# Seam between cross attention and experts: order of the last values, logits and combine weights, earlier splits, and the order of the last pair

## The chip, the cores and the metric

One core of a Trainium2 chip runs the whole kernel in one launch. The metric is the device time in microseconds (us). The engines are TensorE (PE: matrix products and transposes), VectorE (DVE), ScalarE (ACT), GpSimd (POOL) and SyncE (SP), which here only issues the transfers between main memory and on-chip memory. Each engine runs its own list of instructions in order; semaphores make one engine wait for another.

## The reference, cut to what matters

One decoder layer on x of shape (16, 128, 256) in float32, with three residual stages:

```python
x = x + attention(layernorm(x))                    # compressed, selected and window attention
x = x + cross(layernorm(x), context)               # 8 heads, each softmax(q k^T) v over features
x = x + experts(layernorm(x))                      # top 8 of 64 experts, and a shared one

# experts
probs = softmax(x @ gate_w)
topk_w, topk_idx = top_k(probs, 8);  topk_w /= sum(topk_w)
combine = zeros(T, 64).at[arange(T)[:, None], topk_idx].add(topk_w)
for e in range(64):
    out += combine[:, e, None] * ((silu(x @ gw[e]) * (x @ uw[e])) @ dw[e])
out += sigmoid(x @ shared_gate) * shared(x)
```

The kernel computes every expert for every token and weighs it with `combine`, which is zero where an expert was not chosen.

## The kernel before

**Cross attention** goes batch by batch (`B` = 16) through `cross_tensor`, `cross_scalar`, `cross_vector` and `cross_pool`, which list each engine's work in the order in which it runs. A batch has eight score matmuls (u = 0 to 7) whose exponentials ScalarE takes (L1531). `values(b, 0)` and `values(b, 1)` (L1468) are 32 small matmuls that multiply probabilities and values; `keep_pv` (ScalarE, L1546) copies the sums out of their bank; `turn_values` (L1481) transposes them into the bank `XOUT`; `normalised` (VectorE, L1569 and L1571) divides; `turn_back` (L1487) transposes again into the same bank; `residual` (VectorE, L1577) adds to `X`; `next_stats` (L214) begins the next layer norm.

**Routing** takes the batches in four groups of four. `route_turn` (PE, L1686) and `route_split` (VectorE, L1695 and L1697) turn a normalised batch and split it into a high and a low part, because every float32 product is made of three matmuls in the fp32r format (high by high, high by low, low by high). The low parts are made by GpSimd (L1672). `route_logits` (PE, L1707) makes the logits of a batch, `route_keep` (VectorE, L1716) stores them, `route_choose` finds the eight largest (L1730 to L1738), `route_exps` (ScalarE) takes exponentials, `route_weights` (VectorE, L1750 to L1758) makes the combine weights, `route_turn_weights` (PE, L1767) transposes them, `route_keep_weights` (ScalarE, L1774) copies them to `combineT`. SyncE then writes `combineT` to main memory (L1812) and reads single rows back, spread over 64 partitions each, as `comb` (L1817). Of the first pair's `comb`, the half for tokens 0 to 511 needs group 0 and the half for tokens 512 to 1023 needs group 1.

**Experts** are taken as 33 pairs in each of two passes over 1024 tokens, pairs n = 0 to 65; the last pair of a pass holds the shared expert and has only half of the products up. Each pair has two halves h of 512 tokens. On PE, `moe_up` (L1893; L1886 for the shared expert) makes the gate product (side 0) and the up product (side 1) of a half, six matmuls each, and `down` (L1909) twelve matmuls of a half. The PE order is, for a pair n: up(n, 0), down(n-1, 0), up(n, 1), down(n-1, 1). Between them lie, for each half: SiLU on ScalarE (`gate`, L2009), product with the up side on VectorE (`gated`, L2052 into `act_u`; L2050 for the shared expert), product with `comb` on GpSimd (`weigh`, L2109 into `hidden`), the high part on ScalarE (L2015), the low part on VectorE (`hidden_low`, L2057). The weights are split too: high parts on ScalarE (`moe_up_high` L1997, `down_high` L2021), low parts on GpSimd (`moe_up_low` L2099, `down_low` L2114). The hidden values and the weights meet in `down`, which waits for `down_split` and `h_ready`.

In pairs 1 to 13 VectorE also carries the routing of the second eight batches. In pair 1 its order is: gated(1, 0), hidden_low(0, 1), `ln_close` (L245 to L254, the reciprocal square root of the layer norm of batches 8 to 15), gated(1, 1), hidden_low(1, 0), `route_normal` of batch 8 (L259). In pair 2 PE needs that batch for `route_turn` (L1686), which stands between up(2, 0) and down(1, 0).

The order at the seam on PE is `route_logits(7)`, `route_turn_weights(0)`, `turn_values(14)`, `values(15)`, `turn_back(14)`, then the first pair's products up, with `turn_values(15)`, `turn_back(15)` and `route_turn_weights(1)` among them (L1508 to L1522).

Of the kernel before, what the change touches and what calls it, by code (L numbers as in the profile page):

```python
# [8 lines left out]
ALU = mybir.AluOpType  # L9
# [57 lines left out]
def build(nc, io):  # L67
    ctx = ExitStack()
    with ctx:
# [1365 lines left out]
        def cross_tensor(pe):  # L1435
# [56 lines left out]
            for i in range(B):  # L1492
                for u in range(XH):
# [13 lines left out]
                    route_cross_tensor(pe, i, u)  # L1507
            route_logits(pe, 7)  # L1508
            route_turn_weights(pe, 0)
            turn_values(B - 2)  # L1510
            values(B - 1, 0)
            values(B - 1, 1)
            turn_back(B - 2)
            pe.wait_ge(S("x_lo_ready"), ROUTED)
# [3 lines left out]
            moe_up(pe, 0, 0, 0, 0, (1,))  # L1518
            turn_back(B - 1)
            route_turn_weights(pe, 1)  # L1520
            pe.wait_ge(S("x_lo_ready"), 2 * ROUTED)
            moe_up(pe, 0, 0, 0, 1)  # L1522


        def cross_scalar(act):
# [22 lines left out]
            for i in range(B):  # L1548
                for u in range(XH):
                    softmax(i, u)  # L1550
                    if u == 3 and i + 1 < B:
                        cross_keep_shift(act, i + 1)
                    if u == 0 and i + 4 < B:
                        cross_query_high(act, i + 4)
                    if u == 7:
                        keep_values(i)
                    if u == 6 and 0 <= i - 1 < B:
                        keep_pv(i - 1)
                    route_cross_scalar(act, i, u)
            route_keep_weights(act, 0)  # L1560
            keep_pv(B - 1)
            route_exps(act, 1)


        def cross_vector(dve):
# [26 lines left out]
            for i in range(B):  # L1592
# [9 lines left out]
                for u in range(XH):  # L1602
                    if i + 2 < B:
                        cross_reduce_max(dve, i + 2, u)
                    if u == 2 and 0 <= i - 2 < B:
                        normalised(i - 2)
                    if u == 6 and 0 <= i - 2 < B:
                        residual(i - 2)
                    if u == 7 and 0 <= i - 2 < B:
                        next_stats(i - 2)  # L1610
                    route_cross_vector(dve, i, u)
            route_keep(dve, 7)
# [3 lines left out]
            next_stats(B - 2)  # L1616
            normalised(B - 1)
            residual(B - 1)
            route_weights(dve, 1)
            next_stats(B - 1)  # L1620


        def cross_pool(pool):
# [8 lines left out]
            moe_up_low(pool, 0, 0)  # L1632
            route_low_pool(pool, 2 * ROUTED - 1)


# [147 lines left out]
        def route_cross_vector(dve, i, u):  # L1783
# [5 lines left out]
            if (i, u) == (15, 1):  # L1789
                route_choose(dve, 0)  # L1790
            if (i, u) == (15, 5):
                route_weights(dve, 0)

# [103 lines left out]
        def moe_tensor(pe):  # L1897
# [63 lines left out]
            with pe.Fori(0, (PAIRS - 3) // 2) as i:  # L1961
                slot(2 * i + PAIRS + 2, 1, PASS)
                slot(2 * i + PAIRS + 3, 0, PASS)
            slot(LAST, 1, PASS)
            down(LAST, 1, 0)
# [23 lines left out]
        def moe_up_high(act, n, p, ps=0):  # L1989
# [7 lines left out]
            nc.scalar.copy(out, src).then_inc(S("up_hi_ready"), 1)  # L1997

        def moe_scalar(act):
            def up_high(n, p, ps):  # L2000
# [10 lines left out]
            def hidden_high(n, h):  # L2011
                act.wait_ge(S(f"weighed{h}"), n + 1)
                if not isinstance(n, int) or n:
                    act.wait_ge(S("down_done"), 2 * n - 1 + h)
                nc.scalar.copy(h_hi[h][:], hidden[h][:]).then_inc(S(f"h_hi_ready{h}"), 1)  # L2015

            def down_high(n, p):
                act.wait_ge(S(f"ld_down{p}"), 8 * (n - p) + 16)
                if not isinstance(n, int) or n > 1:
                    act.wait_ge(S("down_done"), 2 * n - 2)  # L2020
                nc.scalar.copy(down_hi[p][:], down_in[p][:]).then_inc(S("down_hi_ready"), 1)  # L2021

            def pair(n, p, ps):
# [3 lines left out]
                if not isinstance(n, int) or n:  # L2027
                    hidden_high(n - 1, 1)
                if not isinstance(n, int) or n < LAST:
                    up_high(n + 1, 1 - p, ps)  # L2030
                gate(n, 1)
                if isinstance(n, int) and n in (7, 11):
# [3 lines left out]
                hidden_high(n, 0)  # L2036
                down_high(n, p)

# [4 lines left out]
        def moe_vector(dve):  # L2043
# [16 lines left out]
            def pair(n, p, ps):  # L2060
# [8 lines left out]
                if route:  # L2069
                    route_keep(dve, n + 6)  # L2070
                gated(n, 1, ps)
                if route:
                    route_low(dve, n + 6)
# [22 lines left out]
        def moe_up_low(pool, n, p):  # L2096
            pool.wait_ge(S("up_hi_ready"), n + 1)
            out, src = up_parts(n, up_lo, p)
            nc.gpsimd.tensor_tensor(out, src, up_parts(n, up_hi, p)[0], ALU.subtract).then_inc(S("up_split"), 1)  # L2099

        def moe_pool(pool):
            def weigh(n, p, h):
# [8 lines left out]

            def down_low(n, p):
                pool.wait_ge(S("down_hi_ready"), n + 1)
                nc.gpsimd.tensor_tensor(down_lo[p][:], down_in[p][:], down_hi[p][:], ALU.subtract)\  # L2114
                    .then_inc(S("down_split"), 1)

            def pair(n, p, ps):
                first = isinstance(n, int) and n == 0
                if first:
                    moe_up_low(pool, 1, 1)  # L2120
                weigh(n, p, 0)
                if not first and (not isinstance(n, int) or n < LAST):
                    moe_up_low(pool, n + 1, 1 - p)
                weigh(n, p, 1)
                down_low(n, p)

# [197 lines left out]
```

## Time and profile before

| | |
|---|---|
| median of 3 runs | 1142.57 us (1141.6 to 1144.57) |
| the profiled execution | 1139.89 us |
| its span, first to last instruction | 1138.1 us |
| mean granted TensorE clock | 0.987 of full |
| PE busy | 1068.4 us, 94% |
| VectorE, ScalarE, GpSimd busy | 641.2, 544.4, 639.5 us |
| products up (L1893), three groups of 512 matmuls | 203.4 + 202.4 + 202.0 us |
| products down (L1909), three groups of 528 matmuls | 150.7 + 149.8 + 149.6 us |

The expert stage begins at 557.3 us of the span, with the first matmul of L1893. Cross attention ends around it. A busy time is a sum over an engine's instructions; an engine's idle time matters only if the engine is the one that others wait for at that point. Matmuls are pipelined, so each row's duration overlaps with the next row's start: what a matmul costs is the distance from one start to the next.

### The profile page before, as it was taken

To read this page: it belongs to the slowest core of one execution; us is meant where nothing else is said; L and a number is where in the kernel's file an instruction comes from. 1 tells how busy PE (TensorE), PEld (TensorE's weight loads), DVE (VectorE), ACT (ScalarE), POOL (GpSimd) and SP (SyncE) were. 2 spreads that over 40 slices of the span, in tenths; PEclk is the share of its full clock that TensorE was granted. 3 is DMA by queue.
4 is the path that set the end of the run, shared out by engine and by line. 5 is a ranking of instruction groups with operands and counts; after the bars stand their busy time and mean duration, and the time that the engine had idled before them with its cause. 6 is when DMAs were issued, how large, how long until landed. Compare 5 with 4: busy or idle time off the path is not lost.

```text
span 1138.1 us, 22315 instructions
## 1 busy us (share of the span) xinstructions
PE 1068.4 (94%) x7447; PEld 873.8 (77%) x7480; DVE 641.2 (56%) x1453; ACT 544.4 (48%) x1142; POOL 639.5 (56%) x773
## 2 busy tenths in 40 slices
PE   5979999999999989999799999999999999999997
PEld 4757767777777766766578888888888888888886
DVE  7756777677777779887667643333233323332333
ACT  2326656666666647776433443333343333333332
POOL 4685665656668522222355556665666666656664
PEclk9979999999999999999999999999999999999999
DMA  5201111111100156672143333434435334344342
GB/s 136 66 1 28 31 30 39 32 39 28 40 25 20 38 112 141 155 168 67 40 128 98 98 102 105 126 99 108 118 98 159 105 102 124 97 110 116 97 120 70
DMA packets 75231, 97.10 MB, mean 85 GB/s; under 512 B 20540, under 2 KB 55996, under 8 KB 75148
## 3 DMA queue, kind: packets, MB, share of 16 engines
q1 hardware_dynamic: 75148, 96.05, 32.0%
q8 instruction: 45, 0.74, 0.3%
q14 instruction: 38, 0.31, 0.1%
HBM read 82.73 MB, written 13.12 MB: 84 GB/s over the span
## 4 chain that ended last, share of the span: by engine, by line
PE 56%; DVE 5%; ACT 2%; issue 1%; POOL 0%; POOLq 0%; DVEq 0%; ACTq 0%
PE bank L1893 30%; PE bank L1909 16%; PE bank L1468 2%; PE bank L1443 2%; PE bank L1366 2%; DVE xmax L1376 1%; ACT probs L1531 1%; PE bank L1707 1%; PE bank L1481 1%; PE bank L1886 0%; DVE h_lo L2057 0%; ACT act_g L2009 0%; PE bank L1686 0%; POOL hidden L2109 0%; ACT xpv L1546 0%
## 5 line engine op out<-in xcount | busy, mean ns | idle before, releaser
L2109 POOL TENSOR_TENSOR hidden<-act_u,comb 128x512 f32<-128x512 f32 x132 | 210.5, 1595 | 220.5 <-DVE act_u L2052 152.3
L2052 DVE TENSOR_TENSOR act_u<-act_g,bank 128x512 f32<-128x512 f32 x128 | 88.0, 688 | 335.2 <-ACT act_g L2009 167.6
L2009 ACT ACTIVATE act_g<-bank 128x512 f32<-128x512 f32 x132 | 79.0, 599 | 340.3 <-PE bank L1893 340.2
L1893 PE MATMUL bank<-x_hi,up_hi 128*128 128x512 f32 x512 | 203.4, 397 | 0.1
L1893 PE MATMUL bank<-x_hi,up_lo 128*128 128x512 f32 x512 | 202.4, 395 | 0.0
L1893 PE MATMUL bank<-x_lo,up_hi 128*128 128x512 f32 x512 | 202.0, 394 | 0.0
L1909 PE MATMUL bank<-down_hi,h_hi 128*128 128x256 f32 x528 | 150.7, 285 | 6.3 <-POOL down_lo L2114 6.3
L870 ACT ACTIVATE probs<-bank 128x512 f32<-128x512 f32 x192 | 113.8, 604 | 82.8 <-PE bank L682 45.7
L1909 PE MATMUL bank<-down_hi,h_lo 128*128 128x256 f32 x528 | 149.8, 284 | 0.0
L1909 PE MATMUL bank<-down_lo,h_hi 128*128 128x256 f32 x528 | 149.6, 283 | 0.0
L1893 PEld LDWEIGHTS bank<-x_hi,up_lo 128*128 128x128 f32 x512 | 96.3, 188 | 22.5
L1909 PEld LDWEIGHTS bank<-down_hi,h_hi 128*128 128x128 f32 x528 | 100.8, 191 | 13.6 <-POOL down_lo L2114 8.2
L1893 PEld LDWEIGHTS bank<-x_lo,up_hi 128*128 128x128 f32 x512 | 96.9, 189 | 17.6
L1893 PEld LDWEIGHTS bank<-x_hi,up_hi 128*128 128x128 f32 x512 | 97.1, 190 | 17.0 <-issue 0.3
L2057 DVE TENSOR_TENSOR h_lo<-hidden,h_hi 128x512 fp32r<-128x512 f32 x132 | 103.5, 784 | 7.6 <-ACT h_hi L2015 7.6
L1909 PEld LDWEIGHTS bank<-down_lo,h_hi 128*128 128x128 f32 x528 | 100.8, 191 | 4.8
L1909 PEld LDWEIGHTS bank<-down_hi,h_lo 128*128 128x128 f32 x528 | 101.2, 192 | 0.0
L2099 POOL TENSOR_TENSOR up_lo<-up_in,up_hi 128x512 fp32r<-128x512 f32 (+1 forms) x66 | 87.6, 1328 | 12.2 <-ACT up_hi L1997 12.2
L1531 ACT ACTIVATE probs<-bank 128x512 f32<-128x512 f32 x128 | 75.4, 610 | 39.3 <-PE bank L1443 39.0
L993 DVE TENSOR_REDUCE blockmax<-bank 128x32 f32<-128x512 f32 x96 | 64.7, 689 | 50.6 <-PE bank L632 31.8
L1376 DVE TENSOR_REDUCE xmax<-bank 128x2 f32<-128x512 f32 x128 | 82.3, 683 | 13.7 <-PE bank L1366 13.2
L680 PE MATMUL bank<-query,keys 128*128 128x256 f32 x256 | 84.2, 352 | 0.5 <-ACT probs L870 0.4
(268 smaller groups left out, 2195.7 us busy)
## 6 DMA issues: line engine op xcount, KB each, us to landing
comb<-combine_scratch SPq DMA_DIRECT2D x130, 256.0 KB, 3.8
up_in<-in_w_up SPq DMA_DIRECT2D x66, 256.0 KB, 3.6
down_in<-in_w_down SPq DMA_DIRECT2D x66, 128.0 KB, 3.7
keys_x<-key_rows_x SPq DMA_DIRECT2D x32, 192.0 KB, 3.3
ctx_in<-in_ctx SPq DMA_DIRECT2D x32, 128.0 KB, 2.1
key_rows_x<-ctx_hi SPq DMA_DIRECT2D x256, 16.0 KB, 1.5
query_x<-xq_rows_hi SPq DMA_DIRECT2D x64, 64.0 KB, 3.2
key_rows_x<-ctx_lo SPq DMA_DIRECT2D x128, 16.0 KB, 1.5
```

What stands on the lines that cost most here:

```text
L680: nc.tensor.matmul(o, keys[p][:, kvh * 4 + j, :], query[p][:, kvh, 256:512], start=True, stop=False)
L870: nc.scalar.activation(probs[:, u, :], SCORE[u % 2][:], ACT.Exp, scale=SCALE)\
L993: ins = nc.vector.tensor_reduce(blockmax[:, s, :, c0:c0 + 4], SMAX[m % 2][:].rearrange("p (h c k) -> p h c k", h=KV, k=BLK), AX, ALU.max)
L1376: nc.vector.tensor_reduce(xmax[b % 2][:, m // 4, hs:hs + 2], XMAX[(XH * b + m) % 3][:].rearrange("p (h n) -> p h n", h=2), AX, ALU.max).th ...
L1531: nc.scalar.activation(probs4[b % 2][:, u, :], XSCORE[n % 2][:], ACT.Exp, scale=XSCALE)\
L1893: last = nc.tensor.matmul((GATE, UP)[s][h][:], wp[p][:, c, s, :], xp[:, c, t:t + 512], start=k == 0, stop=k == 5)
L1909: last = nc.tensor.matmul(OUT[k // 2][:, k % 2 * D:k % 2 * D + D], hp[h][:, q * 128:q * 128 + 128], wp[p][:], start=False, stop=True, skip ...
L2009: nc.scalar.activation(act_g[h][:], GATE[h][:], ACT.Silu).then_inc(S(f"gated{h}"), 1)
L2052: ins = nc.vector.tensor_tensor(act_u[h][:], act_g[h][:], UP[h][:], ALU.mult)
L2057: nc.vector.tensor_tensor(h_lo[h][:], hidden[h][:], h_hi[h][:], ALU.subtract)\
L2099: nc.gpsimd.tensor_tensor(out, src, up_parts(n, up_hi, p)[0], ALU.subtract).then_inc(S("up_split"), 1)
L2109: nc.gpsimd.tensor_tensor(hidden[h][:], act_u[h][:], comb[p][:, 512 * h:512 * h + 512], ALU.mult)\
```

## The change

On PE, `values(15)` and `turn_values(14)` go ahead of `route_logits(7)` and `route_turn_weights(0)`; `route_turn_weights(1)` goes behind the gate side of the first pair's second half. On VectorE, `route_weights(0)` leaves its place at (i, u) = (15, 5) and goes behind the last `route_split`, `next_stats` goes behind the `route_split` of the same step, and `route_weights(1)` goes ahead of `residual(15)`. On ScalarE, the high parts of pair 1's weights up and pair 0's weights down are made in the cross stage, and `keep_pv(15)` stands ahead of `route_keep_weights(0)`. On GpSimd, their low parts are made right after the last `route_low_pool`. In the last pair, PE makes both halves up before the two halves down of the pair before; ScalarE splits the down weights between the two SiLUs; VectorE instead of GpSimd makes the product with `comb` for the second half.

```diff
@@ cross_tensor
-            route_logits(pe, 7)
-            route_turn_weights(pe, 0)
             turn_values(B - 2)
             values(B - 1, 0)
             values(B - 1, 1)
+            route_logits(pe, 7)
+            route_turn_weights(pe, 0)
             turn_back(B - 2)
...
             turn_back(B - 1)
+            pe.wait_ge(S("x_lo_ready"), 2 * ROUTED)
+            moe_up(pe, 0, 0, 0, 1, (0,))
             route_turn_weights(pe, 1)
-            pe.wait_ge(S("x_lo_ready"), 2 * ROUTED)
-            moe_up(pe, 0, 0, 0, 1)
+            moe_up(pe, 0, 0, 0, 1, (1,))
@@ cross_scalar
+            moe_up_high(act, 1, 1)
+            moe_down_high(act, 0, 0)
+            keep_pv(B - 1)
             route_keep_weights(act, 0)
-            keep_pv(B - 1)
             route_exps(act, 1)
@@ cross_vector
+                    route_cross_vector(dve, i, u)
                     if u == 7 and 0 <= i - 2 < B:
                         next_stats(i - 2)
-                    route_cross_vector(dve, i, u)
+            route_weights(dve, 0)
             route_keep(dve, 7)
             normalised(B - 2)
             route_choose(dve, 1)
             residual(B - 2)
             next_stats(B - 2)
             normalised(B - 1)
+            route_weights(dve, 1)
             residual(B - 1)
-            route_weights(dve, 1)
             next_stats(B - 1)
@@ cross_pool
             route_low_pool(pool, 2 * ROUTED - 1)
+            moe_up_low(pool, 1, 1)
+            moe_down_low(pool, 0, 0)
@@ route_cross_vector
-            if (i, u) == (15, 5):
-                route_weights(dve, 0)
@@ moe_tensor
-            slot(LAST, 1, PASS)
+            up(LAST, 1, PASS, 0)
+            up(LAST, 1, PASS, 1)
+            down(LAST - 1, 0, 0)
+            down(LAST - 1, 0, 1)
             down(LAST, 1, 0)
             down(LAST, 1, 1)
@@ moe_scalar (down_high is now moe_down_high, outside it)
             def hidden_high(n, h):
-                act.wait_ge(S(f"weighed{h}"), n + 1)
+                if isinstance(n, int) and n == LAST and h:
+                    act.wait_ge(S("last_weighed"), 1)
+                else:
+                    act.wait_ge(S(f"weighed{h}"), n + 1)
...
-                if not isinstance(n, int) or n < LAST:
+                if not isinstance(n, int) or 0 < n < LAST:
                     up_high(n + 1, 1 - p, ps)
+                last = isinstance(n, int) and n == LAST
+                if last:
+                    moe_down_high(act, n, p)
                 gate(n, 1)
...
-                down_high(n, p)
+                if not last and (not isinstance(n, int) or n):
+                    moe_down_high(act, n, p)
@@ moe_vector
                 gated(n, 1, ps)
+                if isinstance(n, int) and n == LAST:
+                    dve.wait_ge(S("ld_comb1"), 16 * LAST + 16)
+                    dve.wait_ge(S("upped1"), LAST + 1)
+                    nc.vector.tensor_tensor(hidden[1][:], act_u[1][:], comb[1][:, 512:1024], ALU.mult)\
+                        .then_inc(S("last_weighed"), 1)
@@ moe_pool (down_low is now moe_down_low, outside it)
-                if first:
-                    moe_up_low(pool, 1, 1)
                 weigh(n, p, 0)
                 if not first and (not isinstance(n, int) or n < LAST):
                     moe_up_low(pool, n + 1, 1 - p)
-                weigh(n, p, 1)
-                down_low(n, p)
+                if not isinstance(n, int) or n < LAST:
+                    weigh(n, p, 1)
+                if not first:
+                    moe_down_low(pool, n, p)
```

## Rows read from the trace of the kernel before

**Rows 1.** Windows: busy us (instructions) of each engine, granted clock, DMA share, GB/s.

```profile
552.20:554.70 2.50, 2.50 (x12) 2.11 (x12) 0.30 (x2) 0.58 (x1) 0.72 (x1) 0.55 0.02 7
...
561.00:563.30 2.30, 0.03 (x2) 0.01 (x1) 2.11 (x8) 0.00 (x0) 0.00 (x0) 1.00 0.00 0
...
572.80:575.50 2.70, 2.67 (x12) 2.67 (x13) 2.67 (x3) 0.62 (x1) 2.48 (x2) 0.52 0.78 187
...
690.00:790.00 100.00, 100.00 (x572) 87.53 (x572) 30.94 (x48) 35.76 (x71) 61.76 (x48) 1.00 0.40 110
```

**Rows 2.** Timeline of TensorE at the seam: start us, duration us, instruction [idle before].

```profile
552.20 0.92 PE L1707 MATMUL bank<-w_router,xnT 128*128 128x65 f32 x4 [3.17 <-DVE xnT L1697]
...
554.75 2.45 PE L1468 MATMUL bank<-probs,xvalue 128*32 128x256 f32 x32
...
558.80 0.60 PE L1481 MATMUL bank<-ident,xpv 128*128 128x128 f32 x4
...
563.29 0.63 PE L1767 MATMUL bank<-ident,combine 128*66 128x128 f32 x4 [2.27 <-DVE combine L1758]
...
572.83 0.53 PE L1909 MATMUL bank<-down_hi,h_hi 128*128 128x256 f32 x1 [2.43 <-POOL down_lo L2114]
...
582.92 0.38 PE L1686 MATMUL bank<-ident,xn 128*128 128x128 f32 x2
```

**Rows 3.** Timeline of ScalarE at the seam.

```profile
549.56 0.37 ACT L1539 COPY xvalue<-bank 128x256 f32<-128x256 f32 x1
...
563.96 0.58 ACT L1774 COPY combineT<-bank 66x512 f32<-66x512 f32 x1 [3.12 <-PE bank L1767]
```

**Rows 4.** Timeline of VectorE at the seam and in pairs 0 and 1.

```profile
549.03 1.40 DVE L1756 TENSOR_TENSOR combine<-chosen,route_s 128x256 f32<-128x256 f32 x1
...
555.50 0.22 DVE L1730 MAX8 top<-logits 128x8 f32<-128x64 f32 x1
...
557.68 0.42 DVE L1577 TENSOR_TENSOR X<-X,bank 128x256 f32<-128x256 f32 x1
...
561.39 0.42 DVE L1750 TENSOR_TENSOR chosen<-chosen,route_e 128x256 f32<-128x256 f32 x1
...
563.05 0.18 DVE L1758 RECIPROCAL combine<-route_e 128x4 f32<-128x4 f32 x1
...
572.78 0.69 DVE L2057 TENSOR_TENSOR h_lo<-hidden,h_hi 128x512 fp32r<-128x512 f32 x1 [2.29 <-ACT h_hi L2015]
...
574.68 1.20 DVE L247 TENSOR_SCALAR rstd<-rstd 128x8 int32<-128x8 int32 x1
...
577.52 0.17 DVE L254 SCALAR_TENSOR_TENSOR rstd<-newton,rstd 128x8 f32<-128x8 f32 x1
...
580.26 1.38 DVE L259 TENSOR_SCALAR xn<-X,mean,rstd 128x256 f32<-128x256 f32 x1
```

**Rows 5.** Timeline of GpSimd at the seam and in pairs 0 and 1.

```profile
548.88 1.26 POOL L2099 TENSOR_TENSOR up_lo<-up_in,up_hi 128x512 fp32r<-128x512 f32 x1
...
570.84 1.26 POOL L2109 TENSOR_TENSOR hidden<-act_u,comb 128x512 f32<-128x512 f32 x1 [3.16 <-DMA comb<-combine_scratch]
...
579.82 1.67 POOL L2109 TENSOR_TENSOR hidden<-act_u,comb 128x512 f32<-128x512 f32 x1 [3.97 <-DVE act_u L2052]
...
581.45 0.78 POOL L2114 TENSOR_TENSOR down_lo<-down_in,down_hi 128x256 fp32r<-128x256 f32 x1
```

**Rows 6.** Timeline of TensorE in the last pair.

```profile
1130.74 0.38 PE L1909 MATMUL bank<-down_hi,h_hi 128*128 128x256 f32 x1 [2.99 <-POOL down_lo L2114]
```

**Rows 7.** Timeline of GpSimd in the last pair.

```profile
1124.88 1.62 POOL L2109 TENSOR_TENSOR hidden<-act_u,comb 128x512 f32<-128x512 f32 x1 [1.70 <-issue]
1128.36 1.65 POOL L2109 TENSOR_TENSOR hidden<-act_u,comb 128x512 f32<-128x512 f32 x1 [1.86 <-DVE act_u L2050]
1129.97 0.72 POOL L2114 TENSOR_TENSOR down_lo<-down_in,down_hi 128x256 fp32r<-128x256 f32 x1
```

**Rows 8.** Timeline of VectorE in the last pair.

```profile
1127.60 0.68 DVE L2050 TENSOR_TENSOR act_u<-act_g,act_u 64x512 f32<-64x512 f32 x1 [2.25 <-ACT act_g L2009]
```

More of the change, by code:

```diff
@@ L1997, in moe_up_high, with moe_down_high @@
             nc.scalar.copy(out, src).then_inc(S("up_hi_ready"), 1)
+        def moe_down_high(act, n, p):
+            act.wait_ge(S(f"ld_down{p}"), 8 * (n - p) + 16)
+            if not isinstance(n, int) or n > 1:
+                act.wait_ge(S("down_done"), 2 * n - 2)
+            nc.scalar.copy(down_hi[p][:], down_in[p][:]).then_inc(S("down_hi_ready"), 1)
         def moe_scalar(act):
@@ L2015, in hidden_high @@
                 nc.scalar.copy(h_hi[h][:], hidden[h][:]).then_inc(S(f"h_hi_ready{h}"), 1)
[L2017 to L2021, printed above, removed]
             def pair(n, p, ps):
@@ L2099, in moe_up_low, with moe_down_low @@
             nc.gpsimd.tensor_tensor(out, src, up_parts(n, up_hi, p)[0], ALU.subtract).then_inc(S("up_split"), 1)
+        def moe_down_low(pool, n, p):
+            pool.wait_ge(S("down_hi_ready"), n + 1)
+            nc.gpsimd.tensor_tensor(down_lo[p][:], down_in[p][:], down_hi[p][:], ALU.subtract)\
+                .then_inc(S("down_split"), 1)
         def moe_pool(pool):
@@ L2110, in weigh @@
                     .then_inc(S(f"weighed{h}"), 1)
[L2112 to L2115, printed above, removed]
             def pair(n, p, ps):
                 first = isinstance(n, int) and n == 0
-                if first:
-                    moe_up_low(pool, 1, 1)
                 weigh(n, p, 0)
```

## The prediction

> **What bounds the kernel now.** I read the page's busy shares first: PE is the only engine near full. Then windows: in the loops of the expert stage PE is busy 100.00 of 100 us, nothing of this change touches the work there, and PE waits for nobody [rows 1]. So the change can only win or lose at the seam and at the end. Next the timeline of PE there. It shows four gaps: 3.17 us before the last logits, ended by VectorE's `xnT`; 2.27 us before the second transposes of combine weights; 2.43 us before the first product down [rows 2]; 2.99 us before the last pair's product down [rows 6]. The windows add the clock: behind the first and the third gap the granted clock was 0.55 and 0.52, the 1.2 GHz level, and behind the second it stayed at 1.00 [rows 1]. Last I read the other engines' timelines, to see what would be late once these gaps close.
>
> All times below are on the axis of the profiled span, those of the changed kernel carried over from rows of before. PE's own pace comes from the loop window: 572 matmuls in 100 us [rows 1], half of them over 512 columns and half over 256, so 0.233 and 0.117 us each; six wide ones are 1.4 us, twelve narrow ones 1.4.
>
> **Seam, first part: up to the second transposes of combine weights.** PE ends its last score at 552.20 - 3.17 = 549.03 [rows 2]. Before, VectorE made combine weights ahead of the last split, and PE's logits hung on that. Now PE does `turn_values(14)` at once (its inputs, `xpv` and `residual(13)`, are there about then), and `values(15)` from 550.0, when ScalarE's `xvalue` has ended (549.56 + 0.37) [rows 3]. The 32 matmuls took 2.38 us (554.75 to 557.13), partly at the low clock; I take 2.1, so 552.1, and the logits end at about 552.65 (under the 0.92 of their row) [rows 2].
>
> VectorE meanwhile: split and `next_stats` to about 550.1, then `route_weights(0)`. Its cost with GpSimd idle is 561.39 to 563.23, 1.84 us [rows 4]. But its L1756 took 1.40 us at 549.03 while GpSimd's L2099 ran from 548.88 to 550.14 [rows 4, 5]; the normal size of such a product over 256 columns is the 0.42 of L1750. The two engines exclude each other. The change puts three more GpSimd products right there: the last x_lo, the low part of pair 1's weights up (1.26) and of pair 0's weights down (0.78) [rows 5], about 2.75 us in a row. Bounds for the end of `route_weights(0)`: 551.95 (no collision) and 553.7 (two collisions of about 0.9). I take 553.15. Then logits kept, `normalised(14)` (0.7) and `turn_back(14)` at 554.15.
>
> The Trainium skill ("SBUF — State Buffer", section "SBUF: two separate sides") has it as a rule that speaks against this part: a VectorE operation with two inputs in SBUF and a GpSimd operation that reads SBUF lock each other out for the whole instruction. The trace agrees, with the 1.40 us above. By the rule in full the end would be 553.7; without it 551.95.
>
> Next a new order bites. `turn_values(15)` needs `residual(14)`, which stands behind `route_choose(1)` on VectorE. Choosing takes from 555.50 to about 557.55, and the residual comes at 557.68 [rows 4]. New: 554.1 + 2.0 = 556.1, residual until 556.5. PE has finished the gate side of half 0 by 555.8 and waits 0.7 us. `turn_values(15)` comes at 556.5 instead of 558.80 [rows 2]: 2.3 us sooner. Behind it PE issues 0.47 of transposes, 1.4 for six matmuls up, 0.23 for `turn_back(15)` and, by the change, another 1.4 for the gate side of half 1, so `route_turn_weights(1)` can start at 560.0. Its weights are ready at 557.8 + 1.84 = 559.65. It started at 563.29 [rows 2]. Gain at this point 3.25 us; the 2.27 us gap is gone, since other work lies in it.
>
> **Seam, second part: the chain through memory.** PE then runs ahead: the rest of the first pair, up(1, 0) until 564.7, the sums started, and down(0, 0) without a wait, because pair 0's weights down are split long before and its hidden values ready at about 563.6. The 2.43 us gap is gone too, and the clock should stay up. But the second half's `comb` still goes ScalarE copy, write, read: from 563.29 to 570.84, 7.55 us [rows 2, 5]. Nothing shortens that; it shifts to 560.05 + 7.55 = 567.6. VectorE's low part of hidden(0, 1) came 1.94 later, at 572.78 [rows 4]: now 569.55, so down(0, 1) starts at 570.3 where PE would be ready at 569.85. That is 8.4 us ahead of the old order, but it does not last. Behind this low part stands `ln_close` on VectorE, which ended at 577.52 + 0.17, 4.91 us after the low part's start, 1.0 of it a wait for GpSimd in L247 [rows 4]. Before, this lay under PE's own work. Now it ends at 569.55 + 4.91 = 574.45, then gated(1, 1), hidden_low(1, 0), and batch 8's normalised rows (L259, 1.38, from 580.26) [rows 4], at 574.45 + 0.7 + 0.6 + 1.4 = 577.15. PE stands ready for `route_turn(8)` at 575.45 (up(2, 0) begins at 572.65, since the second `comb` and the low part of pair 2's weights arrive 3.25 us sooner, not 8), and waits 1.7 us. It ran at 582.92 [rows 2]. GpSimd's `weigh(1, 1)` and `down_lo` (1.67 and 0.78) [rows 5] end at 577.7, and down(1, 0) needs that. It began at 583.08 (582.92 and two transposes). **So 583.08 - 577.7 = 5.4 us are kept.** From there every pair has the phases of before, since PE is the bound. Bounds for this term: below 3.25 less 0.5, if the end of the chain slips as the VectorE and GpSimd products collide in another order; above 7.5, if VectorE's chain is 2 us shorter and PE's own arrival sets it. 5.4 is what the rows' own distances give.
>
> **The end.** Before, the last product down of half 0 waited for hidden(65, 1) and then `down_lo`, both on GpSimd: 1128.36 + 1.65, 1129.97 + 0.72, start at 1130.74 [rows 6, 7]. Now `down_lo` comes right behind hidden(65, 0), 1124.88 + 1.62 = 1126.50 [rows 7], and half 1's SiLU ends at about 1125.95 instead of 1127.57, since up(65, 1) has moved 2.1 us forward on PE. VectorE then has gated(65, 1), blocked to 1126.50, done 1127.05; GpSimd's `down_lo` to 1127.75; the product with `comb` to 1128.35 (sized by its 0.68 neighbour, L2050 [rows 8]); and only then the low part of half 0, which used to be ahead of it in time: 1128.95. Half 1's own low part ends at 1129.7, before PE needs it. PE starts at 1129.0, **1.75 us sooner**. Bounds: 2.9 without any collision, 0.8 with one more of each 1 us.
>
> **Sum.** 5.4 + 1.75 = 7.15 us of the profiled execution's 1139.89, so 1132.7. That execution lies 2.7 below the median of 1142.57, which is what is to be predicted: 1142.57 - 7.15 = 1135.4, say 1135.3. What is costed at nothing: PE's matmuls, which are the same; ScalarE's two early casts, in its idle time before the first combine weights; no transfer is added, and SyncE's order is unchanged.
>
> **Rivals.**
> 1. PE itself sets the restart (the chain through `ln_close` is shorter, because the blocked L247 of 1.20 and L259 of 1.38 [rows 4] would take some 0.2 each where they meet no GpSimd product): 7.5 + 2 to 2.9, about 10 us, 1132.5. For it: both depend on phase alone. Against: GpSimd's products follow the same event, so they shift along.
> 2. The clock falls again. The new waits of PE between 569.8 and 577.7 are about 0.45, 0.9 and 2.0 us; a gap of 2.43 was followed by 0.52, one of 2.27 was not [rows 1, 2]. At the low clock twelve narrow matmuls filled 2.67 us [rows 1] where the pace above gives 1.4, and some three wide ones behind them cost as much again as they take, 0.6: about 1.9 us a time. Gain 7.15 - 1.9 = 5.2, with a second fall 3.3: 1137.4 to 1139.3.
> 3. No change to be seen: `route_weights(0)` beside three GpSimd products ends so late that the second transposes win only 1 us, and the tail's collisions take another 1: gain 3 or less, 1140.
> 4. Slower. The loops leave with other phases, and in every pair the product down waits for `weigh` or `h_lo`, which now collide. It would decide from 7.15/65 = 0.11 us a pair; at 0.2 a pair it costs 13, and 1148 results. Against it: 100.00 of 100 us busy, with GpSimd at 61.76 [rows 1], so about a third of its time is slack, and a PE bound loop pulls the phases back.
>
> **How the numbers follow.** Forecast 0.48, rival 1 0.20, rival 2 0.20, rival 3 0.08, rival 4 0.04. The measurement can tell about 0.3%, 3.4 us, from no change, so faster means below 1139.1: the forecast, rival 1 and most of rival 2, 0.87; same 0.09; slower 0.04. The range 1131.2 to 1139.3 holds the forecast, rivals 1 and 2 and the scatter of the medians, where 1141.6 to 1144.57 was seen.
>
> **What would show it.** Right: no gap above 1 us on PE between 549 and 564, the second transposes (L1767) about 3.2 us sooner, L1893 back to back until the zero matmuls, a wait of 1 to 2 us before L1686 of batch 8 ended by VectorE's `xn`, the granted clock at 1.00 from 549 to 580, and a last gap of about 2 us. Wrong: L1756 at its 0.42 and no wait before L1686 (rival 1), a window at half clock (rival 2), or waits of PE in the loop windows (rival 4).

## The result and the profile after

| | before | changed |
|---|---|---|
| median of 19 runs each | 1141.62 us (1139.28 to 1148.21) | 1137.62 us (1132.01 to 1141.42) |
| ratio, with 95% interval | | 0.9954 (0.9938 to 0.9969) |
| the profiled execution, and its span | 1139.89, 1138.1 us | 1132.01, 1130.2 us |
| mean granted clock of that execution | 0.987 | 0.990 |

Faster, by about 5 us in the runs and by 7.9 us from one profiled execution to the other. A later series gave 0.9933 (0.9920 to 0.9945). Why trace and runs differ is the main thing the experiments had to settle.

TensorE's timeline at the seam in the changed kernel (start, duration, instruction, idle before). L1481 is `turn_values`, L1773 `route_turn_weights`, L1692 `route_turn`, L1897 a product up; it answers to [rows 2].

```profile
548.32 0.39 PE L1692 MATMUL bank<-ident,xn 128*128 128x128 f32 x2
...
548.87 0.65 PE L1481 MATMUL bank<-ident,xpv 128*128 128x128 f32 x4
549.89 1.93 PE L1468 MATMUL bank<-probs,xvalue 128*32 128x256 f32 x32 [0.37 <-ACT xvalue L1540]
...
553.28 0.63 PE L1773 MATMUL bank<-ident,combine 128*66 128x128 f32 x4 [0.86 <-DVE combine L1764]
...
556.52 0.63 PE L1481 MATMUL bank<-ident,xpv 128*128 128x128 f32 x4 [0.68 <-DVE X L1580]
...
560.01 0.60 PE L1773 MATMUL bank<-ident,combine 128*66 128x128 f32 x4
...
569.76 0.34 PE L1913 MATMUL bank<-down_hi,h_hi 128*128 128x256 f32 x1
...
573.24 0.50 PE L1897 MATMUL bank<-x_hi,up_hi 128*128 128x512 f32 x1 [1.82 <-POOL up_lo L2118]
...
576.59 0.41 PE L1692 MATMUL bank<-ident,xn 128*128 128x128 f32 x2 [0.29 <-DVE xn L259]
...
586.11 0.38 PE L1692 MATMUL bank<-ident,xn 128*128 128x128 f32 x2
```

The three gaps of [rows 2] are gone. What is left: 0.37, 0.86 and 0.68 us behind single waits, a new gap of 1.82 before up(2, 0), and 0.29 before batch 8's transposes. The second transposes of combine weights come at 560.01 instead of 563.29, batch 8's at 576.59 instead of 582.92.

VectorE there, against [rows 4]:

```profile
550.99 1.41 DVE L1762 TENSOR_TENSOR combine<-chosen,route_s 128x256 f32<-128x256 f32 x1
552.32 0.69 DVE L1763 TENSOR_SCALAR route_e<-route_e 128x4 f32<-128x4 f32 x1
...
568.98 0.69 DVE L2071 TENSOR_TENSOR h_lo<-hidden,h_hi 128x512 fp32r<-128x512 f32 x1 [3.38 <-ACT h_hi L2031]
...
570.20 1.16 DVE L252 SCALAR_TENSOR_TENSOR newton<-newton,var_eps 128x8 f32<-128x8 f32 x1
...
572.00 1.22 DVE L254 SCALAR_TENSOR_TENSOR rstd<-newton,rstd 128x8 f32<-128x8 f32 x1
...
575.05 1.39 DVE L259 TENSOR_SCALAR xn<-X,mean,rstd 128x256 f32<-128x256 f32 x1
```

and GpSimd, against [rows 5]:

```profile
549.93 0.95 POOL L1678 TENSOR_TENSOR x_lo<-xnT,x_hi 128x256 fp32r<-128x256 f32 x1
550.85 1.27 POOL L2118 TENSOR_TENSOR up_lo<-up_in,up_hi 128x512 fp32r<-128x512 f32 x1
552.08 0.90 POOL L2122 TENSOR_TENSOR down_lo<-down_in,down_hi 128x256 fp32r<-128x256 f32 x1
...
566.99 1.30 POOL L2133 TENSOR_TENSOR hidden<-act_u,comb 128x512 f32<-128x512 f32 x1 [4.55 <-DMA comb<-combine_scratch]
...
571.92 1.26 POOL L2118 TENSOR_TENSOR up_lo<-up_in,up_hi 128x512 fp32r<-128x512 f32 x1 [0.59 <-ACT up_hi L2004]
```

L1762 ends 0.28 us after GpSimd's up_lo (552.40 against 552.12), L1763 0.03 us after its down_lo (553.01 against 552.98). In `ln_close` two operations of eight columns take 1.16 and 1.22 us beside two GpSimd products of 512 columns. From the second transposes to the product with half 1's `comb` it is 566.99 - 560.01 = 6.98 us (7.55 before).

The last pair: TensorE, VectorE, GpSimd, against [rows 6 to 8].

```profile
1122.93 0.36 PE L1913 MATMUL bank<-down_hi,h_hi 128*128 128x256 f32 x1 [1.82 <-DVE h_lo L2071]
```

```profile
1120.09 0.96 DVE L2064 TENSOR_TENSOR act_u<-act_g,act_u 64x512 f32<-64x512 f32 x1 [0.74 <-ACT act_g L2022]
1121.15 1.03 DVE L2089 TENSOR_TENSOR hidden<-act_u,comb 128x512 f32<-128x512 f32 x1
1122.11 1.46 DVE L2071 TENSOR_TENSOR h_lo<-hidden,h_hi 128x512 fp32r<-128x512 f32 x2
```

```profile
1118.88 1.62 POOL L2133 TENSOR_TENSOR hidden<-act_u,comb 128x512 f32<-128x512 f32 x1 [1.68 <-issue]
1120.47 1.17 POOL L2122 TENSOR_TENSOR down_lo<-down_in,down_hi 128x256 fp32r<-128x256 f32 x1
```

From batch 9's transposes to the last products down, 538.59 us before (592.15 to 1130.74), it is now 536.82: 1.77 less, and all of that in the last pair: its first product up begins 529.09 us behind batch 9's transposes before and 529.13 after.

### The profile page after: what moved, and what is told of

Its sections match the earlier page's. It is cut to its first block, busy times and chain, and to the rows that moved or that the text cites. A ratio compares the mean times of both kernels' runs of the same rounds, so it can differ in the third digit from the quotient of the medians.

```text
span 1130.2 us, 22316 instructions
## 1 busy us (share of the span) xinstructions
PE 1068.4 (95%) x7447; PEld 873.1 (77%) x7480; DVE 642.5 (57%) x1454; ACT 544.4 (48%) x1142; POOL 638.0 (56%) x772
## 4 chain that ended last, share of the span: by engine, by line
PE 52%; DVE 4%; issue 3%; ACT 2%; POOL 2%; DMA 1%; SPq 1%; DVEq 0%; ACTq 0%; POOLq 0%
PE bank L1897 29%; PE bank L1913 16%; PE bank L1443 2%; PE bank L1468 2%; PE bank L1366 1%; ACT probs L1532 1%; POOL xn L1673 1%; DVE xmax L1376 0%; POOL x_lo L1678 0%; DMA comb<-combine_scratch 0%; DVE h_lo L2071 0%; PE bank L1481 0%; PE bank L1890 0%; PE bank L1713 0%; SPq L1312 0%
## 5 line engine op out<-in xcount | busy, mean ns | idle before, releaser
L1897 PE MATMUL bank<-x_hi,up_hi 128*128 128x512 f32 x512 | 203.3, 397 | 1.9 <-POOL up_lo L2118 1.8
L1897 PE MATMUL bank<-x_hi,up_lo 128*128 128x512 f32 x512 | 202.5, 395 | 0.0
L1897 PE MATMUL bank<-x_lo,up_hi 128*128 128x512 f32 x512 | 201.8, 394 | 0.0
L1897 PEld LDWEIGHTS bank<-x_hi,up_lo 128*128 128x128 f32 x512 | 96.2, 188 | 22.5
L1897 PEld LDWEIGHTS bank<-x_hi,up_hi 128*128 128x128 f32 x512 | 96.9, 189 | 18.8 <-POOL up_lo L2118 2.0
L1897 PEld LDWEIGHTS bank<-x_lo,up_hi 128*128 128x128 f32 x512 | 96.7, 189 | 17.6
```

What stands on the lines that cost most here:

```text
L1897: last = nc.tensor.matmul((GATE, UP)[s][h][:], wp[p][:, c, s, :], xp[:, c, t:t + 512], start=k == 0, stop=k == 5)
```

## The experiments

Nine kernels, the changed one among them, were timed beside the kernel before, and there is one more trace each of the kernel before, the changed one and splits_only. To compare their traces I use four lengths: A, from the first instruction to the last `route_turn` transposes of the cross stage (548.32 above), in which the kernels differ only in VectorE's order (`next_stats` behind `route_split`, and where the first combine weights begin); the seam, from there to batch 9's transposes (586.11 above); the stretch from there to the last products down; and the rest of the span. The first three come from the same three rows of TensorE's timeline. In the traces that have 8.5 us or more to the end, the granted clock fell to 0.50 behind TensorE's last gap or in the products that follow it.

| trace | A | seam | to last down | to the end | median us, ratio to before |
|---|---|---|---|---|---|
| before | 548.41 | 43.74 | 538.59 | 7.4 | |
| before_again | 548.52 | 43.19 | 538.57 | 9.5 | one run |
| changed | 548.32 | 37.79 | 536.82 | 7.3 | 0.9954 (0.9938 to 0.9969) |
| after_again | 554.28 | 39.20 | 536.80 | 7.3 | 1135.0, 0.9933 (0.9920 to 0.9945) |
| after_third | 551.33 | 37.84 | 536.77 | 7.4 | one run |
| seam_only | 552.49 | 37.90 | 538.58 | 8.7 | 1139.3, 0.9964 (0.9951 to 0.9977) |
| tail_only | 550.07 | 43.53 | 536.77 | 8.7 | 1141.5, 0.9993 (0.9981 to 1.0005) |
| splits_only | 550.20 | 41.31 | 538.57 | 8.7 | 1142.9, 1.0004 (0.9990 to 1.0018) |
| splits_again | 554.97 | 41.05 | 538.60 | 9.6 | one run |
| late_splits | 550.77 | 39.36 | 536.80 | 8.6 | 1138.0, 0.9958 (0.9943 to 0.9972) |
| apart | 548.13 | 38.30 | 536.78 | 7.3 | 1135.0, 0.9940 (0.9923 to 0.9957) |
| tuned | 550.14 | 35.89 | 536.77 | 8.5 | 1133.9, 0.9919 (0.9905 to 0.9932) |
| tuned2 | 551.51 | 35.49 | 536.21 | 7.6 | 1133.4, 0.9923 (0.9906 to 0.9940) |
| fill | 552.67 | 37.86 | 536.78 | 7.4 | 1136.6, 0.9940 (0.9917 to 0.9962) |

**after_again.** The changed kernel, unaltered.

> The changed kernel, unaltered, for a second trace. The two profiled spans differ by 7.9 us (1138.1 and 1130.2), but the timed runs only by a ratio of 0.9954 (0.9938 to 0.9969), some 5.2 us, and its 19 runs spread from 1132.0 to 1141.4 with mean granted clocks from 0.990 down to 0.980. Theory A (clock): runs differ in how long TensorE is at its 1.2 GHz level; time follows the clock at about 10 us per 0.01, and a trace at 1136 or more has half-clock windows that the first one lacked, either somewhere before 545 us (common to both kernels) or between 569 and 578 us, where the gap of 1.82 us stands. Theory B (memory): the chain copy, write, read of the combine weights varies; then the time between the second transposes (L1773) and the product with comb of half 1 (L2133) is not 7.0 us but 9 or more, with the clock at 0.990. Ratio to before expected 0.9954, between 0.993 and 0.998.

Measured: span 1137.6 at a clock of 0.982. The length A is 6 us longer than in the first trace of the same kernel, and there is more half clock in it, most of it early; windows of the first trace and of this one:

```profile
50.00:100.00 50.00, 41.18 (x329) 31.65 (x329) 30.25 (x63) 18.82 (x44) 38.28 (x72) 0.80 0.07 18
```

```profile
50.00:100.00 50.00, 41.68 (x315) 32.17 (x313) 28.32 (x59) 17.14 (x40) 35.85 (x71) 0.73 0.06 16
...
581.00:587.00 6.00, 6.00 (x31) 5.11 (x30) 3.89 (x6) 1.62 (x3) 3.65 (x4) 0.78 0.55 151
```

Between 300 and 400 us the granted clock was 0.97, where the first trace had 1.00. Another 1.4 us are lost in the seam, in a longer gap before up(2, 0) and at the half clock behind it:

```profile
579.80 0.50 PE L1897 MATMUL bank<-x_hi,up_hi 128*128 128x512 f32 x1 [2.52 <-POOL up_lo L2118]
```

Theory A holds; the chain of theory B took 6.88 us here (565.96 to 572.84), no more than in the first trace. The clock's part can be estimated from the runs, each of which has its mean granted clock c. The clock has two levels, so time at the half clock is 2(1-c) times the time. Over the 149 runs that have their clock on record, a straight line within each kernel gives 0.33 us of time per us at half clock. With that part taken out the scatter (standard deviation) of the kernel before (54 runs) falls from 1.8 to 0.8 us and that of the changed one (26) from 2.5 to 0.7, and the kernel before stands at 1130.3, 1130.4 and 1130.2 in the runs timed beside the three later sets:

| | mean us | us at half clock | mean with that part out (error) |
|---|---|---|---|
| before | 1142.9 | 38.5 | 1130.3 (0.1) |
| changed | 1136.8 | 33.9 | 1125.6 (0.1) |
| seam_only | 1139.1 | 34.9 | 1127.6 (0.2) |
| tail_only | 1141.7 | 39.8 | 1128.7 (0.2) |
| splits_only | 1143.2 | 40.3 | 1129.9 (0.2) |
| late_splits | 1137.8 | 34.7 | 1126.4 (0.3) |
| apart | 1135.1 | 30.3 | 1125.2 (0.3) |
| tuned | 1133.4 | 29.8 | 1123.5 (0.2) |
| tuned2 | 1133.6 | 30.6 | 1123.5 (0.3) |
| fill | 1136.8 | 34.5 | 1125.5 (0.3) |

So the change is worth 6.2 us (error 0.5) in the mean of these runs, from the unrounded means. By this estimate 4.7 of them are there with the clock's part out, and 1.5 come through 4.6 us (error 1.4) less at half clock. This takes it that half clock costs the same wherever it lies. Lines through single kernels have slopes of 0.22 to 0.40, which would make the 4.7 anything from 5.2 to 4.3.

**seam_only and tail_only.** The two halves of the change alone; for the first:

```diff
-            up(LAST, 1, PASS, 0)
-            up(LAST, 1, PASS, 1)
-            down(LAST - 1, 0, 0)
-            down(LAST - 1, 0, 1)
+            slot(LAST, 1, PASS)
```

and ScalarE, VectorE and GpSimd of that pair as before; the second is the same edit the other way, in the kernel before.

> The changed kernel with the last pair as before. Theory: seam and end are independent terms. The traces put 6.0 us on the seam and 1.8 on the end, so this kernel should be 1.8 us slower than the changed one, with a last gap on TensorE of 3.0 us again, and the seam up to 580 us as in the changed kernel. Ratio to before 0.9965 if the timed gain is 5.2 us in all, 0.9948 if the seam is worth its 6.0. Rival: the end is worth nothing in time, because the closing stores start when they started before; then it equals the changed kernel.

> The kernel before with only the last pair reordered. Theory: 1.8 us faster than before, ratio 0.9984; last gap on TensorE 1.8 us in place of 2.99, product of half 1 on VectorE delayed by GpSimd's low part to about 1.0 us, its seam unchanged with gaps of 3.17, 2.27 and 2.43. Rival: 0, ratio 1.000.

Measured: with the clock part out, the end is worth 1130.3 - 1128.7 = 1.6 us and the seam 1130.3 - 1127.6 = 2.7 (error 0.2 each), together 4.3 of 4.7: the terms add up. The traces have the end at 1.8 in both (538.58 against 536.8). The intervals of the ratios hold the forecasts of 0.9984 and 0.9965, but tail_only's holds 1 too, so the end's gain shows only with the clock part out, where the rival (the end is worth nothing) falls.

**splits_only and splits_again.** The early splits without the new orders: 

```diff
+            moe_up_high(act, 1, 1)
+            moe_down_high(act, 0, 0)
             route_keep_weights(act, 0)
...
             route_low_pool(pool, 2 * ROUTED - 1)
+            moe_up_low(pool, 1, 1)
+            moe_down_low(pool, 0, 0)
```

> The kernel before with the early splits of pair 1's weights up and pair 0's weights down alone; all orders on TensorE and VectorE, and the last pair, as before. Counted from the last transposes of route_turn in the cross stage (548.41 before, 548.32 after) to those of batch 9 (592.15 and 586.11): before 43.74 us, changed 37.79. Theory: the 2.43 us gap before the first product down and the half clock behind it go, but the chain copy, write, read of half 1's comb and ln_close keep their place; from batch 8's normalised rows (L259, ready at 581.64 at the earliest) TensorE is late again. It starts at 3.17 + 2.27 us of gaps as before, gains 2 to 2.5 us: 41.5. Rival: the gap simply closes in full with its clock and all that follows keeps up: 43.74 - 2.43 - 1.9 = 39.4. Rival 2: another late thing swallows it, 43.7.

> The early splits alone once more. Its first trace was 2.4 us shorter in the seam than the kernel before (41.31 against 43.74), 1.9 of that from a half-clock stretch that was missing, but its runs were not faster (ratio 1.0004, 0.9990 to 1.0018). Theory: the missing stretch was a matter of that execution; in others TensorE falls to 1.2 GHz behind another gap, and only about 0.5 us are kept: 41.3 to 43.5 for the interval. Rival: 41.3 again, and the timed runs lose the 2.4 us elsewhere, in a place where its code is that of the kernel before.

Measured: 41.31 where 41.5 was forecast, and 41.05, just below the 41.3 to 43.5 of the second. As expected the wait moved: in the first trace the first product down no longer waits, the transposes of batch 8 do.

```profile
581.99 0.41 PE L1690 MATMUL bank<-ident,xn 128*128 128x128 f32 x2 [1.35 <-DVE xn L259]
```

But the runs are not faster (1.0004), and with the clock part out 0.4 us are left (error 0.3). The other 2 us of the traces are not found in the runs; the half clock was 40.3 us (error 2.3) against 38.5. The second trace shows a fall behind the 2.27 us gap, where both traces of before had none:

```profile
557.00:569.00 12.00, 8.85 (x64) 5.88 (x64) 7.38 (x33) 4.42 (x11) 2.65 (x3) 0.86 0.14 35
569.00:575.00 6.00, 5.13 (x18) 4.12 (x19) 1.70 (x7) 1.69 (x3) 1.28 (x1) 0.72 0.12 38
```

The first trace of before, behind its gap of 2.27:

```profile
557.00:569.00 12.00, 9.73 (x51) 7.64 (x48) 6.30 (x18) 6.52 (x14) 2.54 (x2) 1.00 0.17 47
```

The seam of splits_again is short all the same. TensorE did not wait before its transposes of batch 8 (586.79), so it seems that the slower products took the time of that wait.

**late_splits.** The new orders without the early splits; the four pieces of work go back to pair 0. The part in the cross stage:

```diff
-            moe_up_high(act, 1, 1)
-            moe_down_high(act, 0, 0)
...
-            moe_up_low(pool, 1, 1)
-            moe_down_low(pool, 0, 0)
```

> The changed kernel without the early splits: pair 1's weights up and pair 0's weights down are split in pair 0 as before; the new orders and the new last pair stay. Theory: pair 1's low part is ready 1.2 us after TensorE wants it, and the product down of pair 0 waits for GpSimd behind the second half's product with comb, a gap of about 3 us before 569 with half the clock behind it: from the last route_turn transposes of the cross stage to those of batch 9 39.5 to 41.5 us instead of 37.79. Rival: since the chain through memory sets the restart anyway, the early splits are worth nothing: 37.8. Second rival: without three GpSimd products beside it route_weights(0) is 1 us shorter, so it is faster than the changed kernel, 37.

Measured: 39.36, 1.6 us more than the changed kernel (the forecast began at 39.5), with two gaps, and a fall of the granted clock behind the second (0.50 from 572.8 to 574.8):

```profile
564.94 0.50 PE L1893 MATMUL bank<-x_hi,up_hi 128*128 128x512 f32 x1 [1.12 <-POOL up_lo L2114]
...
570.81 0.38 PE L1909 MATMUL bank<-down_hi,h_hi 128*128 128x256 f32 x1 [1.94 <-POOL down_lo L2118]
```

and 0.8 us more (error 0.3) with the clock part out. Alone the early splits give 0.4, on top of the new orders 0.8, of 2.7 for the seam: the orders carry most of it.

**apart.** The early low parts wait for the second combine weights.

```diff
+            pool.wait_ge(S("combine_ready"), 2)
             moe_up_low(pool, 1, 1)
             moe_down_low(pool, 0, 0)
```

> The changed kernel, with one wait more: the two early low parts on GpSimd start only when the second combine weights are made, so they no longer stand beside route_weights(0). Theory: L1762 and L1763 take 0.43 and 0.17 us instead of 1.41 and 0.69, combine weights 0 are ready 1.5 us sooner, and the whole VectorE chain behind them (choose, residual, weights 1) with it, of which the second transposes win 0.9 to 1.4 us; from the last route_turn transposes to L1773's second 10.5 instead of 11.69, and to those of batch 9 about 36.8 instead of 37.79. Rival: TensorE's own order holds it (it waited only 0.86 and 0.68 us), gain 0.7 or less, and the late low parts now delay the first products: 37.8 to 38.5.

Measured: the collision is gone,

```profile
550.80 0.43 DVE L1763 TENSOR_TENSOR combine<-chosen,route_s 128x256 f32<-128x256 f32 x1
551.15 0.17 DVE L1764 TENSOR_SCALAR route_e<-route_e 128x4 f32<-128x4 f32 x1
```

and the second transposes stand 11.04 us behind the start of the interval (559.17 - 548.13) where they stood 11.69. But the seam is 38.30, not 36.8: the gap before up(2, 0) is 2.39 and the clock fell behind it. The rival had the size right: 1.5 us of VectorE's wait for GpSimd cost TensorE 0.65 up to there, and 0.4 (error 0.3) in the runs with the clock part out.

**tuned and tuned2.** What the trace of the changed kernel shows as late, moved ahead:

```diff
             normalised(B - 2)
+            residual(B - 2)
             route_choose(dve, 1)
-            residual(B - 2)
-            next_stats(B - 2)
             normalised(B - 1)
             route_weights(dve, 1)
             residual(B - 1)
+            next_stats(B - 2)
             next_stats(B - 1)
...
+            sp.wait_ge(S("up_split"), 1)
+            load_up(2, 0)
             weights_out(1)
```

with `ln_close` in pair 0, and pair 2's high and low parts up ahead of half 1's `comb`. tuned2 adds the wait of apart and puts the low part of half 0 ahead of the product with `comb` in the last pair.

> The changed kernel with what its trace shows as late taken out of the way: residual(14) ahead of choose(1) and next_stats(14) behind the second weights; ln_close of batches 8 to 15 in pair 0, where VectorE waits 3.4 us; the load, the high part and the low part of pair 2's weights up ahead of the second comb. Theory: TensorE's gap of 1.82 us before up(2,0) goes, and the wait before the transposes of batch 8 (0.29) with it; down(1,0) starts at about 574.3 instead of 577.1, so 2.8 us faster than the changed kernel (ratio to before 0.993). Rival 1: the product with comb of half 0 of pair 1 (its comb lands at 570.0) is then last and down(1,0) starts at 576, gain 1. Rival 2: the earlier load takes memory bandwidth from the combine weights and the chain gets as much later, gain 0.

> The version before this one that takes the late things out of the way, with the low parts on GpSimd behind the second combine weights, and in the last pair the low part of half 0 ahead of the product with comb on VectorE. Theory: its wait of 1.26 us before the second product down shrinks to 0.3, from the last route_turn transposes to those of batch 9 35.0 instead of 35.89, and the last gap on TensorE 0.9 instead of 1.82, the end 0.4 us sooner: ratio to before 0.991. Rival: the memory chain (7.0 to 7.4 us from the second transposes to the product with comb) holds everything and nothing is won, ratio as measured for the former, 0.992.

Measured: the seam is 35.89 and 35.49, 1.9 and 2.3 less than the changed kernel. What ends the one gap of tuned between the seam's second transposes and batch 9 is now the chain through memory:

```profile
572.45 0.39 PE L1916 MATMUL bank<-down_hi,h_hi 128*128 128x256 f32 x1 [1.26 <-DVE h_lo L2076]
```

Both beat the kernel before and stand 2.1 us under the changed one with the clock part out, between the 2.8 of the theory and the 1 of rival 1. Between the two there is no difference in the runs (0.0, error 0.3): tuned2's last gap shrank from 1.82 to 1.24 + 0.22 and its seam by 0.4, but its rival, that the chain through memory holds everything, fits the ratio.

**fill.** Six matmuls of no use in each of the two largest gaps, before up(2, 0) and before the last products down.

```diff
+            def fill(out):
+                for _ in range(6):
+                    nc.tensor.matmul(out[:], x_hi[:, 0, 0:128], x_hi[:, 0, 0:512], start=True, stop=True)
```

> The changed kernel with six matmuls of 512 columns whose result is thrown away in each of its two largest gaps: before up(2,0) and before the last pair's products down. They take 1.4 us of gaps of 1.8 to 2.5 us. Theory: TensorE's clock no longer falls behind these gaps; nothing else changes, so the trace has 1.00 from the seam to the end, the interval to batch 9's transposes is 37.8, the end (last products down to the last instruction) 7.3, and the mean time is 0.5 to 1 us less than the changed kernel's, ratio to before about 0.993. Rival: the fill delays the real matmuls that would have run sooner in some executions, or the clock stays up anyway, and nothing is gained.

Measured: no fall from the seam to the last product in the trace, and no gain in the runs: 34.5 us at half clock against 33.9, 1125.5 against 1125.6, and both 1136.8 in the mean (error 0.7). The rival fits; a gain of 0.5 us is not excluded.

**before_again and after_third.**

> The kernel before once more, for a second trace of it. Theory: TensorE's instructions and waits at the seam repeat (3.17, 2.27, 2.4 us), and the half-clock stretches do not: they lie at other places from execution to execution, most of them ahead of the seam. From the last route_turn transposes of the cross stage to those of batch 9: 43.7 if both stretches (behind the first and the third gap) are there again, 1.9 less for each that is not, and the start of that interval between 548 and 555 us. Rival: both stretches are a fixed property of these gaps, 43.7 within 0.2.

> The changed kernel a third time. Interval from the last route_turn transposes of the cross stage to those of batch 9: 37.8 in its first trace (gap before up(2,0) 1.82, clock 1.00), 39.2 in its second (gap 2.52, clock down to 0.78 behind it). Theory: the length of that gap follows the landing of pair 2's weights up, and the clock falls behind a gap over about 2.3 us; 37.8 to 39.3. The start of the interval between 548 and 555.

Measured: 43.19 and 37.84. In before_again both stretches of half clock in the seam were there again, at the same places; so the theory that they move was wrong for them, and its seam is shorter because the third gap was only 1.83 us. The clock fell behind that gap nevertheless. It also fell behind the last gap of 2.99, where the first trace of before, whose window stands last here, had 1.00:

```profile
572.39 0.39 PE L1909 MATMUL bank<-down_hi,h_hi 128*128 128x256 f32 x1 [1.83 <-POOL down_lo L2114]
```

```profile
569.00:575.00 6.00, 4.10 (x19) 3.11 (x19) 4.19 (x12) 1.51 (x3) 4.14 (x4) 0.83 0.90 231
...
1130.20:1134.50 4.30, 4.22 (x19) 4.22 (x20) 1.95 (x3) 0.00 (x0) 0.03 (x1) 0.50 0.00 0
```

```profile
1130.70:1133.00 2.30, 2.26 (x19) 2.26 (x20) 1.21 (x2) 0.00 (x0) 0.00 (x0) 1.00 0.00 0
```

In after_third the gap before up(2, 0) was 2.37 and the clock stayed. So the length of a gap does not say whether the clock falls behind it; my expectation of a limit near 2.3 us was wrong.

## Why the prediction was right, point by point

- **What bounds**: shown. From batch 9 to the last pair nothing moved (538.57 to 538.60 with the old end, 536.77 to 536.82 with the new one; 536.21 in tuned2, which changes the last pair again).
- **Seam, first part**: forecast 552.1 for the end of `values(15)`, 553.15 for weights 0, 556.5 for `turn_values(15)`, 560.0 for the second transposes; measured 551.8, 553.2, 556.52 and 560.01. The wait of VectorE for GpSimd was foreseen and a little larger: L1762 and L1763 took 1.41 and 0.69, together 1.5 more than their 0.43 and 0.17 in apart, where 1.2 were put in the sum. By the rule of the Trainium skill ("SBUF — State Buffer", section "SBUF: two separate sides") a VectorE operation with two inputs in SBUF and a GpSimd operation that reads SBUF lock each other out for the whole instruction. The traces agree for L1762, which ended 0.28 us after GpSimd's product.
- **The chain through memory**: forecast 567.6, measured 566.99.
- **What ends the restart**: the waits were foreseen in kind, and their sizes were off against each other. Forecast were a wait of 0.45 before the second product down, 0.9 before up(2, 0) and 1.7 before batch 8's transposes; measured 0, 1.82 and 0.29. A wait of 1 to 2 us before those transposes was named as a sign of being right, and it did not come. The term that was mis-sized is the landing of pair 2's weights. They were asked for 3.3 us sooner, as forecast, but ScalarE could begin their high part 5.5 us after that instead of 4.4 (6.0 and 6.1 in the other two traces of the changed kernel, with gaps of 2.37 and 2.52). The trace of before had a wait for them, on ScalarE, that the prediction passed over. Before, then changed:

```profile
569.05 0.59 SPq L1804 DMA_DIRECT2D up_in<-in_w_up  x1
573.41 0.62 ACT L1997 CAST up_hi<-up_in 128x512 fp32r<-128x512 f32 x1 [0.66 <-DMA up_in<-in_w_up]
```

```profile
565.75 0.59 SPq L1808 DMA_DIRECT2D up_in<-in_w_up  x1
571.23 0.62 ACT L2004 CAST up_hi<-up_in 128x512 fp32r<-128x512 f32 x1 [2.28 <-DMA up_in<-in_w_up]
```

  Why they land later is open: tail_only, whose seam is that of before, took 5.8 us for the same. The chain of `ln_close` was sized right (4.84 us from its low part's start, 4.91 forecast), and batch 8's rows were ready at 576.44, 0.7 sooner than forecast, mostly because the chain through memory was 0.6 shorter.
- **The seam's sum**: 5.4 forecast, 5.95 in the first pair of traces. The three traces with the seam of before have 43.19 to 43.74, the four with the new one (changed and seam_only) 37.79 to 39.20; their means differ by 5.3. That the parts come so near in sum is in part luck, since the errors in the waits had opposite signs.
- **The end**: 1.75 forecast, 1.77 measured, 1.6 in the runs. The steps came as forecast too: the product up waits for GpSimd's `weigh`, and the low part of half 0 comes last.
- **The sum**: 7.15 forecast; 7.9 from trace to trace, 5.2 (3.5 to 7.1) and 7.65 (6.3 to 9.1) in the two series, 6.2 in the mean of all runs with a clock on record. The median itself was forecast at 1135.3 and came at 1137.62, which is inside the stated range, but where rival 2 stood (1137.4 to 1139.3). The two series of the changed kernel, 1137.2 and 1135.8 in the mean, are at 1125.6 and 1125.6 with the clock part out, and differ in their time at half clock, 35.1 and 31.1 us. The forecast booked the half clock of the old seam as won in full: that seam has 6.7 us of it (windows of 12, 6 and 6 us at 0.86, 0.83 and 0.89, the same in both traces of before). In the new seam it was gone in two traces of three, and the runs save 4.6 us (error 1.4) in the mean. The early splits, which take the third gap away, save none that the runs show.
- **Rival 2** (the clock falls again) happens in some executions of the changed kernel: 1 of 3 traces. Rivals 3 and 4 fall: the second transposes came 3.28 us sooner, and the stretch to the last pair did not change. Rival 1's extra gain is what tuned gets in part; it took L259 at 0.2 us where no GpSimd product meets it, and the median of its 24 executions in the trace of before is 0.41.

What stays open is what decides whether the clock falls behind a given gap, and why the early splits alone leave the time at half clock as it was; the traces are too few for either.

## What to carry to other kernels

Where a new order closes gaps, follow each other engine's list past the gap: here a lead of 8.9 us at the second product down (569.76 for 578.69) shrank to 6.0 within one pair, by a chain that had lain hidden under TensorE's own wait. A single trace is one draw of the clock; with each run's mean clock at hand, take that part out before you compare, and book a half-clock stretch as won only in part where a new gap takes the old one's place. Look for the waits of the other engines, too, that cost nothing yet: here ScalarE's wait for pair 2's weights grew from 0.66 to 2.28 us and stands behind TensorE's new gap of 1.82. Put GpSimd's products where VectorE's chain is not what TensorE waits for, but ask how much of VectorE's wait reaches TensorE: here 0.65 of 1.5 us.

## What the runs showed of the hardware that was not expected

- VectorE operations of eight columns, normally 0.17 us, took 1.16 and 1.22 while GpSimd ran a product of 512 columns. Which of a chain's small operations is caught depends on the kernel and the execution: L245 and L247 in both traces of before, L252 and L254 in the first of the changed kernel, L254 twice in its second, L250 and L252 in its third.
- The length of a gap does not say whether the granted clock falls behind it. It fell behind gaps of 1.83 us (before_again) and 1.94 (late_splits), and stayed at 1.00 behind 2.27 (before) and 2.37 (after_third). Behind the same last gap of 2.99 us it stayed at 1.00 in before and was 0.50 in before_again.
- The stretch A took 548.3 to 554.3 us in three executions of one kernel, the changed one, and 548.1 to 555.0 over all traces. Between 50 and 100 us the granted clock was 0.80 in the shortest and 0.73 in the longest.
